# GpSimd subtracts each weight's mean in four operations of 256 columns instead of one of 1024

## What is computed

```python
x = x + xattn(layernorm(x), pos, ctx, ...)      # the attention layer, several small parts
x = x + ffn(layernorm(x), w1, mean_w1, w2, mean_w2, w3, mean_w3)

def binary_diff_weight(w, base):
    d = w - base
    coeff = mean(abs(d))                        # one number for the whole matrix
    return base + coeff * sign(d)

W1, W2, W3 = (binary_diff_weight(w, mean_w) for each of the three pairs)
h = silu(x @ W1.T) * (x @ W3.T)                 # 1024 -> 3584 features
return h @ W2.T                                 # 3584 -> 1024
```

## Time and profile before

| | us |
|---|---|
| median of three runs | 1272.66 (1272.12 to 1275.04) |
| the profiled execution: its time | 1270.68 |
| its span, first to last instruction | 1268.9 |
| busy: TensorE | 1185.2 |
| busy: DVE | 981.4 |
| busy: ACT | 694.1 |
| busy: GpSimd | 283.4 |

### The profile page before, as it was taken

How to read it: one execution, slowest core, us unless ns; L and a number is a source line. 1 busy time by engine, 2 the same in 40 slices (tenths; PEclk the granted TensorE clock), 3 DMA queues, 4 the chain that set the end, 5 groups by cost and what they waited for, 6 DMA issues and landing times. The chain is left out here.

```text
span 1268.9 us, 17072 instructions
## 1 busy us (share of the span) xinstructions
PE 1185.2 (93%) x6298; PEld 921.5 (73%) x6298; DVE 981.4 (77%) x1287; ACT 694.1 (55%) x999; POOL 283.4 (22%) x187
## 2 busy tenths in 40 slices
PE   5889878898899599999999999999999999999998
PEld 3755455565666478888878888887788888888887
DVE  6878678867787957988887778797786777888864
ACT  4768566574455547565566655565564334334342
POOL 2223223323331212334133333232340000000000
PEclk9999999999999699999999999999999999999999
DMA  9266667865011145768667778766795877853232
GB/s 358 91 243 248 253 242 264 309 245 188 13 67 67 50 149 143 227 220 277 215 216 224 230 240 265 208 203 192 234 287 165 316 279 255 283 198 122 95 126 107
DMA packets 99062, 257.35 MB, mean 203 GB/s; under 512 B 9362, under 2 KB 23972, under 8 KB 98468
## 3 DMA queue, kind: packets, MB, share of 16 engines
q1 hardware_dynamic: 94948, 241.59, 52.7%
q0 software_dynamic: 4032, 14.68, 6.4%
HBM read 214.81 MB, written 41.42 MB: 202 GB/s over the span
## 5 line engine op out<-in xcount | busy, mean ns | idle before, releaser
L2004 ACT ACTIVATE split<-grid 128x1024 fp32r<-128x1024 f32 x98 | 104.0, 1061 | 160.8 <-PE pair L1542 147.4
L2468 POOL TENSOR_TENSOR raw_w<-raw_w,raw_base 128x1024 f32<-128x1024 f32 x56 | 143.5, 2579 | 214.7 <-DMA raw_base<-in_mean_w 214.2
L2412 DVE TENSOR_TENSOR split<-grid,split 128x1024 fp32r<-128x1024 f32 x98 | 119.6, 1224 | 61.9 <-ACT split L2004 61.7
L1542 PE MATMUL quad<-split 128*128 128x512 f32 x588 | 149.3, 389 | 0.5 <-DVE hid L2419 0.5
L1542 PE MATMUL pair<-split 128*128 128x512 f32 x588 | 149.2, 389 | 0.0
L1542 PEld LDWEIGHTS quad<-split 128*128 128x128 f32 x588 | 110.3, 188 | 23.7 <-DVE split L2412 0.9
L1542 PEld LDWEIGHTS pair<-split 128*128 128x128 f32 x588 | 110.4, 188 | 22.9
L1501 PE MATMUL pair<-xnT_hi,ring_hi 128*128 128x512 f32 x224 | 88.1, 393 | 9.6 <-DVE t_b_lo L2215 9.6
L1501 PE MATMUL pair<-t_b_hi,ring_hi 128*128 128x512 f32 x224 | 88.9, 397 | 4.4 <-ACT snap L1968 4.1
L2183 DVE TENSOR_TENSOR ring_lo<-raw_base,ring_hi 128x1024 fp32r<-128x1024 f32 x56 | 68.3, 1220 | 26.4 <-ACT ring_hi L1949 21.0
L1501 PE MATMUL pair<-xnT_hi,ring_lo 128*128 128x512 f32 x224 | 87.9, 392 | 0.0
(11 more groups left out here) (332 smaller groups left out, 2784.8 us busy)
## 6 DMA issues: line engine op xcount, KB each, us to landing
raw_w<-in_w SPq DMA_DIRECT2D x56, 512.0 KB, 5.4
raw_base<-in_mean_w SPq DMA_DIRECT2D x56, 512.0 KB, 6.7
grid<-h_blocks SPq DMA_DIRECT2D x49, 512.0 KB, 3.7
ctxw<-in_w SPq DMA_DIRECT2D x28, 512.0 KB, 4.0
ctxw<-in_mean_w SPq DMA_DIRECT2D x28, 512.0 KB, 5.2
late<-in_mean_w SPq DMA_DIRECT2D x28, 512.0 KB, 7.5
late<-in_w POOLq DMA_DIRECT2D x28, 512.0 KB, 6.2
grid<-in_mean_w SPq DMA_DIRECT2D x28, 512.0 KB, 4.7
```

What stands on the lines that cost most here:

```text
L1542: a = pe.matmul(into[t], found[:, a, t * P:(t + 1) * P], found[:, b, :], start=p == 0 and n == 0 and q < 4, stop=p == PAIRS - 1 and n == 2 ...
L2004: act.activation(splits[n % RINGS][:, 0:2, :], operands(n), ACT.Copy).then_inc(a_hi, 1)
L2412: dve.tensor_tensor(found[:, 2:4, :], operands(n), found[:, 0:2, :].bitcast(F32), ALU.subtract).then_inc(a_lo, 1)
L2468: pool.tensor_tensor(w[:, :], w[:, :], base[:, :], ALU.subtract).then_inc(f_diff, 1)
```

## The change

A constant says four; a helper makes the difference in that many operations on adjacent columns and returns the last; both users of GpSimd's difference call it and attach their signal to the last operation. The wait for the load stands ahead of the first, as before. It concerns 18 differences of the measurement (14 on `ctxw`, 4 on `big`) and 56 of weight rows, 4 of these in the attention layer; the differences that DVE makes stay whole. Lines behind the constant are one higher after the change, those behind the helper eight.

```diff
+QUARTERS = 4
...
+            def subtract(w, base):
+
+                for n in range(QUARTERS):
+                    some = slice(n * HID // QUARTERS, (n + 1) * HID // QUARTERS)
+                    a = pool.tensor_tensor(w[:, some], w[:, some], base[:, some], ALU.subtract)
+                return a
+
             def measure(t):
                 w, base = measured(t)
-                pool.tensor_tensor(w, w, base, ALU.subtract).then_inc(me_pool, 1)
+                subtract(w, base).then_inc(me_pool, 1)
 
             def difference(n):
                 w, base = raws[n % ROWS]
                 pool.wait_ge(ld_raw[n % ROWS], 32 * (n // ROWS + 1))
-                pool.tensor_tensor(w[:, :], w[:, :], base[:, :], ALU.subtract).then_inc(f_diff, 1)
+                subtract(w, base).then_inc(f_diff, 1)
```

## The result

The changed kernel takes 1262.23 us (median of five runs, 1261.08 to 1265.67) against 1272.89 for the kernel before (five runs, 1272.12 to 1278.08): a ratio of 0.9913, with a 95% interval from 0.9887 to 0.9938. It is faster by 0.9%, some 10.7 us. The forecast was 1271.5 with a range of 1266 to 1277, so it was wrong: too small by nearly all of the gain.

What follows compares the result with a forecast made beforehand. TensorE bounds the FFN, a dependent chain through all engines the attention layer. Attention -2.2 and FFN +1.0 give -1.2 us on the profiled 1270.68: 1269.5, as a median 1271.5 from 1272.66, range 1266 to 1277.

Steps and rivals of the forecast that it cites:

- the taking of turns: DVE and GpSimd alternate at quarter ends: DVE waits at most about 0.7 us instead of 2.35; differences may be interrupted.
- Rival 3: All divided differences: DVE gets no turn between quarters, each hold lasts 2.79 us; +4.4 us, 1277.1; chance 0.09.
- The attention layer's term, -2.2: Attention layer: four shortened DVE holds less two longer differences on the chain, -2.2 us together, ends -6 and +1.
- At 314 us: Attention layer, hold at 314.45: DVE in 1.5 us earlier, later quarters delay its next two-input operation about 0.4: -1.1 us.
- At 324.87: Attention layer: DVE's L2157 runs between the differences, L2160 stands a quarter more, ending at 327.7 instead of 328.76: about -1.0.
- At 332.00: Attention layer: small operation gains 1.5 us, but L2157 and L2160 take turns with later quarters: -0.2 us.
- At 44.80: Attention layer's early hold: DVE's small operation ends 1.5 us earlier; half counted because 390 us of other waits follow: -0.8.
- The +0.9 for two differences on the chain: Attention layer, before 277.26 us and about ten us earlier: two differences holding nothing of DVE get longer, +0.9 us.
- The measurement's part: Attention layer, the measurement's differences: the early hold's -0.8 us and the +0.9 for two longer differences on the chain.
- The FFN's term, +1.0: FFN: gaps at 870 and 910 us -0.4 each, 638 us +0.3, 594 us +1.5; +1.0 us, from -1.5 to +5.
- The feared loss at 594 us: FFN: DVE's turn of 1.21 us inside a difference ends it 1.65 later, with no cover before TensorE's product: +1.5 us.
- Rival 1: Refunds of the four attention-layer holds arrive whole, 1.6 us each; -6.3 us, 1266.4, or 1267.2 as taken; chance 0.34.

Runs made afterwards that it cites:

- four adds held: Kernel before, differences whole; only the adding transfers behind rows 36, 40, 44 and 48 held until after the next row's load: 1271.96 us, ratio 0.9979.
- the measurement alone: Kernel before with only the measurement's 18 differences in quarters, all 56 weight rows whole: 1270.70 us, ratio 0.9974.
- the loads behind: Changed kernel, all differences in quarters, with SyncE's loads of rows 41, 45 and 49 made to wait longer: 1272.75 us, ratio 1.0002 against the kernel before.
- the adds late: Kernel before, differences whole, with GpSimd's adding transfer behind every fourth FFN row held until after the next row's load: 1287.26 us, ratio 1.0106.

## Why the prediction was wrong

**What bounds it, and the taking of turns: right, but for two places.** Four undisturbed quarters take 2.82 us (2.79 worked out), and DVE's 128x3 operation is held 0.67 us (under 0.85). Rival 3, no turn between quarters, is refuted by that as the rule for this kernel. It is not for every place. In the changed kernel's trace eight quarters that follow directly on the issue of `wadd` gave DVE no turn: its subtraction (1.23 us where nothing holds it) stood until they were done, and TensorE's one remaining wait for `snap` comes behind it:

```profile
702.80 0.89 POOL L2528 DMA_DIRECT2D late<-in_w  x1 [8.54 <-ACT late L1981]
703.42 5.86 POOL L2466 TENSOR_TENSOR raw_w<-raw_w,raw_base 128x256 f32<-128x256 f32 x8
...
704.37 5.99 DVE L2184 TENSOR_TENSOR ring_lo<-raw_w,ring_hi 128x1024 fp32r<-128x1024 f32 x1 [1.56 <-ACT ring_hi L1815]
...
712.17 0.50 PE L1502 MATMUL pair<-t_b_hi,ring_hi 128*128 128x512 f32 x1 [0.72 <-ACT snap L1969]
```

At 670.44 us a DVE operation stood 3.1 us in the same way beside four quarters. In both places a quarter lasts 1.03 us and the next starts 0.33 before its end; elsewhere an undisturbed one lasts 0.72 and the overlap is 0.03. What the Trainium skill states of consecutive Pool instructions ("GPSIMD Engine Reference", "2.1 Instruction dispatch") does not decide who gets the shared access in between: the 0.67 us and the 5.99 us show both.

**The attention layer's term, -2.2: mis-sized.** Of the 4.82 us in these two traces, 3.55 come at the first four weight rows, and 0.47 are there at 40 us, before anything divided has run. The steps, against the differences of starts of before and after:
- At 314 us: -1.1 forecast, -1.0 measured (offset -1.05 before it, -2.05 at 322.66).
- At 324.87: -1.0 forecast, -1.5 measured. At 332.00: -0.2 forecast, -1.06 measured. The step that failed is "two-input operations take turns, so the second ends only 0.1 to 0.2 earlier". DVE's first (L2158) did not wait at all: it went on where the small one had ended, 0.95 us at 329.07, and only the next stood, for 0.41:

```profile
328.41 4.28 POOL L2466 TENSOR_TENSOR raw_w<-raw_w,raw_base 128x256 f32<-128x256 f32 x4
...
328.47 0.68 DVE L2033 SCALAR_TENSOR_TENSOR stat_back<-stat_back 128x2 f32<-128x2 f32 x1 [0.82 <-POOL stat_back L2460]
329.07 0.95 DVE L2158 TENSOR_TENSOR hid<-hid,wr_a 128x768 f32<-128x768 f32 x1
330.05 1.37 DVE L2161 TENSOR_TENSOR hid<-hid,wr_q 128x768 f32<-128x768 f32 x1
```

  I had let a quarter in between every two of DVE's operations. But DVE's L2158 starts 0.08 us before the small one ends, and it was GpSimd's second quarter that stood behind it. Three holds gave 3.55 us where I had 2.3.
- At 44.80 the gain of 1.6 us is there in every trace with a divided measurement (table above). Whether it lasts was set by something else. In four of the eight, after's among them, TensorE's clock was granted at the lower of its two levels (1.2 GHz) for 3.4 us at 55 us and the 1.6 us were gone by 83; in the other four it stayed at 2.4 GHz there, and in them the gain stood until at least 118 us. The lower level can be had without the change too (the trace with four adds held, 6.8 us at 54.8). The stretch in after and in the kernel with the 768-column operations divided (from:to, length, busy PE, PEld, DVE, ACT, POOL, clock):

```profile
55.50:58.90 3.40, 3.40 (x23) 3.00 (x20) 3.33 (x7) 2.34 (x4) 0.56 (x1) 0.50 0.00 0
```

```profile
55.50:58.90 3.40, 3.32 (x36) 2.72 (x37) 3.23 (x5) 2.95 (x5) 0.00 (x0) 1.00 0.03 11
```

  What TensorE did just before doesn't tell them apart: from 50 to 55 us it was busy for 2.78 us in after and for 2.77 with the measurement alone, where the clock stayed. Half of it, my guess, is then right as a mean, by luck. A further 0.8 to 1.9 us that the work between 228 and 253 us takes less in all eight traces with a divided measurement (0.1 more in four with a whole one) I had not seen.
- The +0.9 for two differences on the chain: not seen as a loss in any trace, but not separable either. The measurement's part was +0.1 in the sum and is -3.0 (-5.3 to -1.4) in time. Of that the traces show 0 or 1.6 early and about 0.9 at 240 us.

**The FFN's term, +1.0: wrong sign, and the wrong mechanism.** The step that failed is the latency of the load: I carried the 9.7 us from issue to difference at 856.39 over unchanged, and moved only its start, by 0.87 us (2.5 measured, 0.6 of them TensorE's). It was long because GpSimd's adding transfer had been issued just ahead. The load now overtakes that transfer, which the longer difference, to me a cost of 0.44 us, keeps from coming as much earlier. In the four rows of the table the load gains 2 to 4 us by it. So the gaps of 2.06 and 0.88 us went wholly and not by 0.4 each. That of 1.15 at 638 us, to which I gave +0.3, went as well, and one of 0.72 came at 712 (above). The feared loss at 594 us did not come: row 17's difference met no turn (2.83 us) and ended 2.3 us earlier against the FFN's start. The FFN's part is 2.0 us in time (+0.3 to -4.7 by the interval, so not shown), 1 to 5 us by the traces; before's own profile is at the slow end of what whole differences show (555.8 to 559.7), which is why a comparison of two traces alone made it look as large as the attention layer's.

**The rivals.** Rival 1, the refunds arrive whole, is nearest: it had -6.3 us, of which the attention layer's holds are now -3.55 and -1.6 (the latter lost again in the trace of after), and the FFN came on top. Its chance of 0.34 was too low: the rows for it (ACT standing 2.06 us right behind a held operation) were on the page, and I set against them turns that I had not seen in a row.

**Left open:** what makes up the rest of the measurement's 3.0 us, if its interval leaves one. It may lie in the FFN: with whole FFN differences its first half took 555.8 us in both traces with a divided measurement, and 558.9 and 559.7 in the two with a whole one, which may as well be scatter. On the other side, in five of the eight traces with a divided measurement, and in none of the five others, TensorE's clock was granted at 1.2 GHz for 3.4 to 13.7 us from 214 to 218 us on, and 0.8 to 3.0 us were lost there. Open too: why the clock falls there and at 55 us in some executions, and why DVE got no turn in some places behind `wadd`. None of it was tried.

## What to carry to other kernels

A long GpSimd operation with SBUF operands beside a chain of small two-input DVE operations costs the chain up to its whole length, so cut it into pieces of about the length that the chain can bear. Of the three sizes tried here 0.7 us was best; at 0.45 us nothing was left of the gain, and in the FFN, where each piece is a place for DVE to step in, ACT waited for the differences more than twice as long. Look at the trace whether the chain really gets in: here it did not where the pieces came directly behind the issue of a transfer on GpSimd. When a profile shows a load that takes 9 us where its like takes 5, look at what was issued in the microsecond ahead of it before taking the latency as given: who is first is a thing that an edit elsewhere can turn round. And read one trace's gaps only beside a second trace of a kernel with the same code there.

## What the runs showed of the hardware

- In rows 37, 41, 45 and 49 a load of two times 512 KB issued 0.3 to 1.1 us behind GpSimd's adding transfer of 512 KB took 6.2 to 9.3 us to its user, issued 0.9 to 3.4 us ahead of it 4.5 to 5.6 (52 loads in 13 traces). Other rows differ: row 16, 0.3 behind, 5.6.
- A waiting DVE operation mostly gets in at the end of the running GpSimd operation (0.67 us instead of 2.29), and DVE's next one can follow without giving way. Where GpSimd's operations followed directly on its issue of a transfer and overlapped by about 0.33 us, a DVE operation stood until all eight were done (5.99 us at 704.37 in after, 6.86 at 744.79 with the loads behind); beside three whole differences it stood until they were done as well (7.88 us at 488.15 with the adds late), but in before one got in between two of them (2.30 us at 710.77). GpSimd's longest quarter lasted 1782 ns, 722 of its own and the rest DVE's turn.
- A GpSimd subtraction of two f32 operands costs about 0.17 us and 2.12 ns a column: shortest on `raw_w` 1264 ns for 512 columns, 722 for 256, 446 for 128.
